# The first stretch of a three-stage decoder layer: fold stores issued one by one, a value tile moved, first maxima in two sets of banks

## The reference

```python
x = _layernorm(x + attention(x, Wq, Wkv_down, Wk_up, Wv_up))       # 16 heads of 32, latent 128, rotary, causal
x = _layernorm(x + cross(x, W_qkv, W_o, ctx, ctx))                 # top 54 of 512 scores kept, softmax
x = _layernorm(x + experts(x, Wg, Wu, Wd, Ga..Db, Wr))             # 8 experts, the first 2 with low-rank additions
```

## Time and profile before

| | |
|---|---|
| median of 3 runs | 1687.88 us (1686.06 to 1693.19) |
| profiled execution, its own time | 1688.87 us |
| its span | 1687.0 us |
| PE busy | 1480.7 us (88%) |
| DVE busy | 1199.2 us (71%) |
| ACT busy | 908.2 us (54%) |
| POOL busy | 777.4 us (46%) |
| DMA, mean over the span | 44 GB/s |

### The profile page before, as it was taken

One profiled execution on the slowest core, in us unless ns is written; L12 is line 12 of the kernel. 1 busy time (PEld: TensorE's weight loads), 2 busy tenths in 40 slices (PEclk: granted clock), 3 DMA queues, 4 the chain that ended last, 5 costly groups with the idle time before them and its releaser, 6 DMA issues.

```text
span 1687.0 us, 27697 instructions
## 1 busy us (share of the span) xinstructions
PE 1480.7 (88%) x10404; PEld 907.4 (54%) x10404; DVE 1199.2 (71%) x2027; ACT 908.2 (54%) x1463; POOL 777.4 (46%) x685
## 2 busy tenths in 40 slices
PE   5859797878878898848799999999999999999984
PEld 2435656556644455423456655666566655666553
DVE  3737687787648999976867767667667767767757
ACT  3417576675554445446555565555555565556542
POOL 5408264451122223687644664556454654456411
PEclk9759898998669999969899999999999999999997
DMA  9050010002111110120001001001001001100002
GB/s 275 34 197 4 29 51 2 28 26 73 55 50 51 50 51 26 51 76 1 25 26 38 26 26 38 26 26 38 26 26 38 26 26 31 33 26 27 12 1 100
DMA packets 68148, 74.68 MB, mean 44 GB/s; under 512 B 9008, under 2 KB 46512, under 8 KB 66992
## 3 DMA queue, kind: packets, MB, share of 16 engines
q1 hardware_dynamic: 67440, 68.68, 12.6%
q10 hardware_dynamic: 576, 4.19, 0.6%
HBM read 49.66 MB, written 10.49 MB: 36 GB/s over the span
## 4 chain that ended last, share of the span: by engine, by line
PE 66%; DVE 15%; issue 10%; ACT 5%; POOL 2%; SPq 1%; DMA 1%; DVEq 0%; ACTq 0%; POOLq 0%
PE banks L1135 48%; PE banks L894 7%; DVE nmf L1517 2%; PE banks L999 2%; PE banks L948 2%; PE banks L962 2%; PE banks L983 2%; ACT pf L1225 1%; DVE top L1641 1%; DVE wk L1637 1%; DVE attf L1648 1%; DMA w_fold<-w_top 1%; PE banks L964 1%; PE banks L985 1%; PE banks L1090 1%
## 5 line engine op out<-in xcount | busy, mean ns | idle before, releaser
L1135 PE MATMUL banks<-xc,w 128*128 128x512 f16 x2688 | 592.3, 383 | 17.9 <-ACT banks L1176 15.1
L1135 PEld LDWEIGHTS banks<-xc,w 128*128 128x128 f16 x2688 | 264.5, 99 | 340.2 <-ACT banks L1176 20.2
L1135 PE MATMUL banks<-wd,mid 128*128 128x256 f16 x2688 | 298.1, 273 | 5.7 <-ACT banks L1176 3.1
L1135 PEld LDWEIGHTS banks<-wd,mid 128*128 128x128 f16 x2688 | 263.6, 98 | 41.2 <-ACT banks L1176 3.4
L871 POOL TENSOR_TENSOR mid<-m,mid 128x512 f16<-128x512 f32 x64 | 75.1, 1173 | 319.7 <-ACT mid L1176 319.7
L1176 ACT ACTIVATE banks<-banks 128x512 f32<-128x512 f32 x192 | 108.6, 578 | 192.9 <-PE banks L1135 192.9
L871 POOL TENSOR_TENSOR mid<-msum,mid 128x512 f16<-128x512 f32 x128 | 186.0, 1471 | 2.6 <-ACT mid L1176 2.6
L1464 DVE SCALAR_TENSOR_TENSOR w<-stage,w 128x512 f16<-128x512 f32 (+1 forms) x56 | 61.4, 1135 | 106.1 <-ACT w L1176 106.1
L1517 DVE TENSOR_REDUCE nmf<-banks 128x1 f32<-128x512 f32 (+3 forms) x256 | 107.4, 480 | 27.1 <-PE banks L964 26.4
L1176 ACT ACTIVATE mid<-msum 128x512 f16<-128x512 f32 x128 | 81.0, 633 | 84.5 <-DVE msum L1822 28.3
L778 POOL TENSOR_TENSOR plo<-pf,phi 128x1280 f16<-128x1280 f32 x24 | 63.2, 2641 | 119.3 <-ACT phi L1176 118.9
(11 more groups left out here) (256 smaller groups left out, 3023.8 us busy)
## 6 DMA issues: line engine op xcount, KB each, us to landing
stage<-w_fold SPq DMA_DIRECT2D x24, 256.0 KB, 3.0
stage<-in_Wg SPq DMA_DIRECT2D x24, 256.0 KB, 3.2
stage<-in_Wu SPq DMA_DIRECT2D x24, 256.0 KB, 3.1
stage<-in_Wd SPq DMA_DIRECT2D x24, 256.0 KB, 2.8
vcat<-vnext SPq DMA_DIRECT2D x8, 528.0 KB, 3.3
x_in<-in_x SPq DMA_DIRECT2D x4, 1024.0 KB, 6.5
x_res<-in_x SPq DMA_DIRECT2D x4, 1024.0 KB, 5.5
c_raw<-in_ctx SPq DMA_DIRECT2D x4, 1024.0 KB, 5.7
```

Source lines behind the costliest of these rows:

```text
L1135: mm = nc.tensor.matmul(out, l(x, i), r(y, i), start=start and i == 0 and j == 0, stop=stop and i == k - 1 and j == 2, skip_group_check=True)
```

## The change

It edits only the first stretch:

- SP issues each fold's store right behind that fold, in order, and the two value moves after the last store.
- `v.3` on PE, ACT and DVE goes from behind `maxn.3` to the rows: on PE behind `row.5`, on ACT behind `row.5`, on DVE behind `v.2`. A list `A_FIRST_PE` gives the first stretch its own order for the bank waits.
- `bqn.1` and `bqn.3` of the first stretch write `st_ps` instead of `max_ps`, and `bqn.1` to `bqn.3` wait for the maxima one head less far; `maxn.1` and `maxn.3` read there.
- POOL makes the own rows after its eight `rope` steps instead of before them.

```diff
 A_START_PE = steps("""
-    row.5 turn.4 fold.3 row.6 turn.5 fold.4 row.7 fold.5
+    row.5 v.3 turn.4 fold.3 row.6 turn.5 fold.4 row.7 fold.5
...
-    fold.0 fold.1 row.0 c.0 row.1 rhi.0 row.2 rhi.1 row.3 v.0 fold.2 rhi.2 row.4 rhi.3 v.1 fold.3 v.2 row.5 rhi.4 fold.4
-    row.6 rhi.5 fold.5 row.7 rhi.6 rhi.7 k0.0 k0.1 k0.2 k0.3 v.3
+    fold.0 fold.1 row.0 c.0 row.1 rhi.0 row.2 rhi.1 row.3 v.0 fold.2 rhi.2 row.4 rhi.3 v.1 fold.3 v.2 row.5 v.3 rhi.4 fold.4
+    row.6 rhi.5 fold.5 row.7 rhi.6 rhi.7 k0.0 k0.1 k0.2 k0.3
...
-    half.0 half.1 c.0 rlo.0 rlo.1 fold.0 v.0 rlo.2 half.2 fold.1 v.1 rlo.3 half.3 fold.2 v.2 rlo.4 half.4 fold.3 rlo.5
+    half.0 half.1 c.0 rlo.0 rlo.1 fold.0 v.0 rlo.2 half.2 fold.1 v.1 rlo.3 half.3 fold.2 v.2 v.3 rlo.4 half.4 fold.3 rlo.5
     half.5 fold.4 fold.5 q0.0 q0.1 q0.2 rlo.6 rlo.7 q0.3 maxn.0 maxn.1 maxn.2
-    maxn.3 v.3 mTn.0 maxn.4
+    maxn.3 mTn.0 maxn.4
...
+A_FIRST_PE = [u for u in A_START_PE if u[0] not in ("turn", "fold")]
+A_FIRST_PE += [u for u in next_part(A_PE, A_NEXT) if u not in A_FIRST_PE]
...
+        def max_bank(b, i):
+
+            return st_ps if b is None and i in (1, 3) else max_ps
...
             store_fold(0)
             sp.wait_ge(cat_stored, 16)
+            for n in range(1, 6):
+                store_fold(n)
             sp.wait_ge(a_drained["v"], a_upto(0, ("v", TT - 1)))
             move_values(0, 0)
             move_values(0, 1)
-            for n in (5, 4, 1, 2, 3):
-                store_fold(n)
             sp.wait_ge(fold_stored, 5 * 16)
...
             heads(next_part(A_POOL, A_NEXT), None, 0)
+            pool.wait_ge(roped, 2 * TT * 4 + FREE)
+            own_row = kcT[K3:K3 + G, :, :].rearrange("p (g j) n -> p g j n", j=G)
+            pool.memset(kcT[K3:K3 + G, :, :], 0.0).then_inc(own_rows, 1)
+            pool.wait_ge(own_rows, 1)
+            pool.affine_select(out=own_row, in_=own_row, compare_op=ALU.not_equal, fill=SNM, base=0,
+                               pattern=[[0, H // G], [-1, G], [0, S]], channel_multiplier=1).then_inc(own_rows, 1)
+            pool.wait_ge(own_rows, 2)
...
-                        pe.wait_ge(max_done, (own * H + i) * 4 + FREE)
+                        free = i - 1 if b is None and 0 < i < G else i
+                        pe.wait_ge(max_done, (own * H + free) * 4 + FREE)
+                        score = max_bank(b, i)
...
-                            nc.vector.tensor_reduce(nmf[:, t, i % G:i % G + 1], max_ps[:, o:o + w], AX, ALU.max, negate=True)\
+                            nc.vector.tensor_reduce(nmf[:, t, i % G:i % G + 1], max_bank(b, i)[:, o:o + w], AX, ALU.max, negate=True)\
```

More of the change, by code:

```diff
@@ L746, in _ @@
                                pattern=[[1, P]], channel_multiplier=-1).then_inc(consts, 1)
-            own_row = kcT[K3:K3 + G, :, :].rearrange("p (g j) n -> p g j n", j=G)
             pool.wait_ge(consts, 15)
[L750 to L755, removed]
             pool.wait_ge(cossin_loaded, 16)
@@ L961, in heads @@
                             o = OFF[t + 1]
-                            nc.tensor.matmul(max_ps[:, o:o + w], qcT[0:K3, i, t * P:(t + 1) * P], kcT[0:K3, i, 0:w],
+                            nc.tensor.matmul(score[:, o:o + w], qcT[0:K3, i, t * P:(t + 1) * P], kcT[0:K3, i, 0:w],
                                              start=True, stop=False)
-                            mm = nc.tensor.matmul(max_ps[:, o + w - P:o + w], identb[:, :], mask_qk[:, :],
+                            mm = nc.tensor.matmul(score[:, o + w - P:o + w], identb[:, :], mask_qk[:, :],
                                                   start=False, stop=True)
@@ L1029, in _ @@
                 else:
-                    at = next_part(A_PE, A_NEXT).index(u)
-                    heads(next_part(A_PE, A_NEXT), None, 0, [], at, at + 1)
-            at = next_part(A_PE, A_NEXT).index(("q0", 0))
+                    at = A_FIRST_PE.index(u)
+                    heads(A_FIRST_PE, None, 0, [], at, at + 1)
+            at = A_FIRST_PE.index(("q0", 0))
             pe.wait_ge(lora_added, 24)
-            heads(next_part(A_PE, A_NEXT), None, 0, [], at)
+            heads(A_FIRST_PE, None, 0, [], at)
             for k in ("xT", "c", "row", "v", "q0", "k0"):
```

## The result

The changed kernel takes 1668.8 us (median of 5 runs, 1660.18 to 1670.96) against 1690.56 us (median of 5, 1686.06 to 1693.19): a ratio of 0.9875, 95% interval 0.9852 to 0.9899. The forecast was 1669, range 1661 to 1676.

What follows compares the result with a forecast made beforehand. The prediction took the first stretch to be a chain of waits; -5.7 + 2.6 + 4.7 - 5.8 - 13.4 - 1.0 = -18.6 us took 1688.9 to 1670.3, and the median, 1.0 lower, to 1669 us, range 1661 to 1676.

Steps and rivals of the forecast that it cites:

- The stall: Before the batch body, DVE's wait for a store goes: -13.4 us of PE idle time, -1.0 us for PE's clock.
- The front: At the start, DVE's low part of wq is no longer held by POOL's select, so row.0 starts earlier: -5.7 us.
- v.3: Among the rows, PE waits 1.9 us for the drain of v.2 and computes 0.7 us: +2.6 us.
- The hold of row 6: Behind the rows, POOL's moved select starts 0.8 us before DVE's rlo.6 and holds it: +4.7 us.
- The first rival: Behind the rows, rlo.6 comes before the select, so the 4.7 us are not lost: 1664.6 us, chance 0.25.
- The memset: At the moved own rows, POOL's memset, which only writes, would not hold rlo.6; taken from the skill, no row showing it.
- The maxima: First five heads: with two bank sets PE and DVE stop alternating, -5.8 us: 5.1 by the banks, 0.7 by v.3.
- The rest of the kernel: Stages B and C keep their code and only start earlier as a whole: 0 us.
- rivals 3 and 4: Rival 3: before the body, DVE meets another wait ending near the old time, 1683.7 us, chance 0.05. For the other see rival 4.
- rival 4: In the batch loop, a longer spell of PE at 1.2 GHz makes it slower; a whole batch at least 1719 us; chance 0.04.
- rival 2: At the front, its gain is lost because the folds or their factors become late: 1675 us, chance 0.12.

Runs made afterwards that it cites:

- e1: The changed kernel with SP's order alone undone (value moves first, then stores 5, 4, 1, 2, 3), v.3 staying among the rows: 1668.5 us.
- e5: The changed kernel with v.3 back behind maxn.3 and SP's old order (value moves, then stores 5, 4, 1, 2, 3): 1681.4 us.
- the repetition: The changed kernel run once more, nothing edited, for a second profile and more times: 1669.2 us; its profiled execution had a span of 1669.4.
- e11: The kernel before with SP's new order alone (each store behind its fold, value moves last): 1672.4 us against 1689.1.
- e3: The changed kernel with all first maxima in banks 0 to 2 and the waits of before, v.3 staying among the rows: 1672.9 us.
- e10: The changed kernel with the memset before the first rope, the select behind rlo.7 and v.3 back behind maxn.3: 1660.2 us.
- e2: The changed kernel with the own rows (memset and select) back before the first rope: 1667.7 us, ratio 0.9883.
- e8: The changed kernel with the memset before the first rope and POOL's select waiting for the copy of q0.1, to meet rlo.6: 1666.9 us.
- e4: The changed kernel with v.3 back behind maxn.3, the stores staying behind their folds: 1666.6 us, ratio 0.9889.

## Why the prediction was right

- **The stall**, -14.4 us forecast with the clock behind it: -15.0 to -15.4. Its cause as stated was right, and its size; with the clock it gave 0.6 to 1.0 us more than I took, well inside the ends. What the prediction missed is that the new place of `v.3` frees the stores as well (`e1`), so the edit of the order is one of two that do the same; only without both is the stall back (`e5`).
- **The front**, -5.7: -5.68 at `row.0`. Not all of it arrived. In the repetition `row.6` was only 0.65 us earlier than before, where 3.1 were due. Of the 2.4 us between, 0.7 went in the product of `row.0`, which took 5.28 us instead of 4.54, and 1.7 in the rows behind it, which had 7 us of 1.2 GHz where before there were 3.4 (in the profiled one 2.67 arrived). This is the term that was over-sized in the typical execution, by 2.4 us, and it had no line in my sum. Part of it is the reference: `e11`, whose rows are those of the kernel before, had no 1.2 GHz among them and started `row.6` at 57.41 us, 2.1 earlier than the trace that the forecast was made from.
- **v.3**, +2.6: from the start of `row.5` to that of `turn.4` 3.25 us against 0.65 before, in both executions: 2.6.
- **The hold of row 6**, +4.7 with a margin of 0.8 us: 4.63, met with that margin. The first rival, at 0.25, is the case of one trace and, by the times, of 3 of 11. (Where the prediction turns to the Trainium skill it calls this rival the second; it is the first of its list.) I named a higher clock as what would bring it, but gave it 1664.6; it came at 1660, since the clock that lets `rlo.6` win also shortens the stretch from `q0.0` to `maxn.0` by 3.4 us beyond the hold. As a separate price for a separate event it was mis-sized: cause and effect come together.
- **The memset** lets an operation with two SBUF inputs pass: `rlo.6` took 0.68 us in the profiled execution, all of it inside the memset. That is what the Trainium skill says ("SBUF — State Buffer", section "Who interferes with whom"), and now a trace shows it; its other half, that an operation of POOL which reads SBUF holds them, is shown by 7.96, 6.85, 7.02 and 5.23 us.
- **The maxima**, -5.8: -5.88 in the trace, 5.3 by undoing the banks alone (`e3`; 5.1 forecast) and 0.57 for `v.3` (`e10`; 0.7 forecast).
- **The rest of the kernel**, 0: -0.8 and -1.2. Nothing was lost there in these two executions, and no trace of the changed kernel speaks for rivals 3 and 4. That rival 4's mechanism exists is shown by `e2`, at 5 to 7 us; the prediction's "at least" 50 us for a whole batch is worked out from no row. Something of rival 2's kind did happen (2.4 us of the front), but by the clock and not by late weights.

The forecast for the median came within 0.2 us, partly by luck. The over-sized front (2.4 us) stands against the stall and the rest, 1.4 us better than reckoned. The forecast for the difference was -18.6 us; against the median of before as it stands with five runs, 1690.56 instead of the 1687.88 that I started from, it is -21.8. The time fits to 0.2 us and the difference only to 3, and that is the scatter of the reference.

## What to carry to other kernels

Before moving work of POOL that reads SBUF, list what DVE does with two SBUF inputs at both places: here the move took 5.7 us from one hold and gave 4.6 back to another, and a wait that keeps the select behind the rows got them for nothing. When a store or load queue is late, look for the one wait at its head; freeing what it waits for and reordering the queue are the same gain, not two. Where two events are a microsecond apart in the profile, expect either order, and take more than one profile before explaining one. A difference of medians that equals a forecast term is no proof of it: follow it through the steps of both traces, as `e2` shows.

## What the runs showed of the hardware

- The granted clock of PE falls at different places in executions of one and the same kernel: at 78.0 us in one, at 68.5 in the other, with the same instructions; in the first stretch alone this moved a step by 3.4 us. What picks the place was not tried.
- An operation held by POOL started (in the trace) when it was issued and ended 0.54 us after POOL's (84.10 after 83.56 in the repetition, 82.56 after 82.02 in `e8`, and the same in `e1`, `e4` and `e5`), so it was held to the select's end each time, however late it had come.
- Five stores of 1 MB issued together landed within 16.5 us (71.0 to 87.5), about 320 GB/s; one with no other transfer beside it (those of folds 1 to 3 in the changed kernel) in 4.3 to 4.8 us.
